# A ring of weight blocks, filled block by block instead of in four parts

## The reference

```python
h = silu(xn @ W1 * s1) * (xn @ W2 * s2)      # 256 -> 1024
h = gelu(h @ H1 * t1)                        # 1024 -> 1024
h = gelu(h @ H2 * t2)                        # 1024 -> 1024
ffn = h @ W3 * s3                            # 1024 -> 256
out = x + attention + ffn
```

## Time and profile before

| | |
|---|---|
| median of 3 runs | 1600.02 us |
| lowest, highest | 1595.21, 1600.1 us |
| profiled execution | 1599.94 us |
| its span | 1598.1 us |
| PE busy (matmuls) | 1520.8 us, 95% |
| DVE busy | 1169.4 us, 73% |
| ACT busy | 946.9 us, 59% |
| POOL busy | 481.8 us, 30% |
| DMA traffic | 298.16 MB, 84963 packets |
| of it GpSimd's queue | 238.04 MB, 37152 packets |

### The profile page before, as it was taken

The page is one execution under the profiler, slowest core; times in us unless marked ns, Lnnn a source line. Parts: engine busy times, 40 slices in busy tenths (PEclk is TensorE's granted clock), DMA queues, the critical chain, the costliest instruction groups (busy, mean ns, idle before and its releaser), DMA issues.

```text
span 1598.1 us, 33158 instructions
## 1 busy us (share of the span) xinstructions
PE 1520.8 (95%) x10956; PEld 1431.3 (90%) x10956; DVE 1169.4 (73%) x2087; ACT 946.9 (59%) x1745; POOL 481.8 (30%) x569
## 2 busy tenths in 40 slices
PE   7756999999999999999999999999999999999996
PEld 4756899998999999899999989999998999999896
DVE  4744686877868687786868778686877868686775
ACT  3523465665656566565656656565665656565563
POOL 1321051332405133240513324051332405133240
PEclk8977999999999999999999999999999999999999
DMA  8787356382745638274563827456382745737262
GB/s 298 257 302 265 120 174 236 101 274 75 256 153 170 235 103 272 77 256 153 169 234 104 268 81 256 153 165 236 106 267 82 257 152 163 239 105 249 88 228 86
DMA packets 84963, 298.16 MB, mean 187 GB/s; under 512 B 7232, under 2 KB 44224, under 8 KB 59584
## 3 DMA queue, kind: packets, MB, share of 16 engines
q0 software_dynamic: 37152, 238.04, 44.6%
q1 hardware_dynamic: 47344, 58.49, 11.3%
q10 hardware_dynamic: 432, 1.18, 0.2%
HBM read 280.91 MB, written 23.07 MB: 190 GB/s over the span
## 4 chain that ended last, share of the span: by engine, by line
PE 84%; DVE 6%; DMA 4%; issue 3%; ACT 2%; SPq 1%; POOL 1%; DVEq 0%; ACTq 0%; POOLq 0%
PE ps L833 48%; PE ps L808 13%; PE ps L862 8%; PE ps L713 4%; PE ps L714 4%; PE ps L715 4%; PE ps L753 2%; DMA weight_blocks<-in_w_ffn 2%; DVE values_a L1268 1%; DVE operands_a L1276 1%; DMA weight_set<-in_w_ffn 1%; PE ps L764 1%; PE ps L774 1%; PE ps L723 1%; DMA weight_blocks<-weight_set 1%
## 5 line engine op out<-in xcount | busy, mean ns | idle before, releaser
L833 PE MATMUL ps<-operands_a,hidden_weights 128*128 128x256 f32 x5376 | 697.8, 284 | 30.1 <-DVE operands_a L1276 13.4
L833 PEld LDWEIGHTS ps<-operands_a,hidden_weights 128*128 128x128 f32 x5376 | 665.4, 191 | 35.6 <-DVE operands_a L1276 17.0
L1299 DVE TENSOR_TENSOR partial_sums<-partial_sums,ps 128x512 f32<-128x512 f32 x320 | 218.1, 686 | 192.3 <-PE ps L833 128.8
L1276 DVE TENSOR_TENSOR operands_a<-values_a,operands_a 128x512 fp32r<-128x512 f32 x336 | 252.4, 770 | 57.6 <-POOL values_a L612 45.8
L618 POOL DMA_DIRECT2D hidden_weights<-weight_blocks x252 | 140.6, 558 | 495.9 <-PE ps L833 417.8
L833 PE MATMUL ps<-operands_b,hidden_weights 128*128 128x256 f32 x1792 | 256.8, 287 | 23.4 <-issue 11.2
L833 PEld LDWEIGHTS ps<-operands_b,hidden_weights 128*128 128x128 f32 x1792 | 233.4, 193 | 28.0 <-issue 18.0
L808 PE MATMUL ps<-xnT,w_ffn 128*128 128x512 f32 x1024 | 253.3, 399 | 0.0
L808 PEld LDWEIGHTS ps<-xnT,w_ffn 128*128 128x128 f32 x1024 | 189.3, 189 | 42.0
L1015 ACT ACTIVATE operands_a<-values_a 128x512 fp32r<-128x512 f32 x192 | 117.2, 628 | 70.3 <-POOL values_a L612 22.4
L1042 ACT ACTIVATE values_out<-partial_sums,vectors 128x256 f32<-128x256 f32 x192 | 87.0, 502 | 107.3 <-DVE partial_sums L1299 107.3
(11 more groups left out here) (108 smaller groups left out, 2076.7 us busy)
## 6 DMA issues: line engine op xcount, KB each, us to landing
hidden_weights<-weight_blocks POOLq DMA_DIRECT2D x192, 1024.0 KB, 5.3
hidden_weights<-weight_blocks POOLq DMA_DIRECT2D x64, 512.0 KB, 4.1
raw_weights<-weight_blocks SPq DMA_DIRECT2D x48, 272.0 KB, 2.7
x<-in_H SPq DMA_DIRECT2D x16, 512.0 KB, 5.5
weight_set<-in_w_ffn SPq DMA_DIRECT2D x16, 512.0 KB, 9.7
out_dram<-acc SPq DMA_DIRECT2D x32, 256.0 KB, 2.2
weight_blocks<-in_w_ffn SPq DMA_DIRECT2D x12, 512.0 KB, 14.7
weight_blocks<-weight_set SPq DMA_DIRECT2D x4, 1536.0 KB, 5.1
```

The costliest lines, as they stand in the source:

```text
L833: r = mm(bank[:, m * HT:(m + 1) * HT], ring_weights[:, place, 2 * g + j, m * P:(m + 1) * P], as_used(buf[:, j, slot[block_of_b], part, :]) ...
L1276: v.tensor_tensor(lo_part(group, block), value(group, block), hi_part(group, block).bitcast(F32), ALU.subtract).then_inc(lo_half.sem, 1)
L1299: v.tensor_tensor(scratch[:, dst, :], scratch[:, kept, :], product_bank(s, i), ALU.add).then_inc(add.sem, 1)
```

## The change

The ring gets seven parts of one block each, each with its own semaphore. Every refill waits for the one product whose block it replaces, and GpSimd's list has seven refills a step. They stand in groups where the four stood; in steps 1 and 3, where the products run in another order than the ring, the list follows the products' order, and in step 1 the refills of blocks 6 and 2 (R 1.2 and R 1.4) stand ahead of T4 of H0, the one of block 5 (R 1.1) behind it, with 7, 3 and 4.

```diff
 RING_ORDER = (1, 5, 6, 7, 2, 4, 3)
-RING_PARTS = ((0, 1), (1, 2), (3, 2), (5, 2))
-PART_OF = {1: 0, 5: 1, 6: 1, 7: 2, 2: 2, 4: 3, 3: 3}
+RING_PARTS = tuple((at, 1) for at in range(PRODUCTS))
+PART_OF = {i: at for at, i in enumerate(RING_ORDER)}
...
-PART_FREE = ((1, 6, 2, 3), (1, 5, 7, 4), (1, 6, 7, 3), (1, 5, 7, 4))
+PART_FREE = (RING_ORDER,) * SETS
...
                         refill(t, 0, 1)
                         refill(t, 0, 2)
+                        refill(t, 0, 3)
+                        refill(t, 0, 4)
                     t1(t, "H0")
                     t2(t, "H0")
                     if filling:
-                        refill(t, 0, 3)
+                        refill(t, 0, 5)
+                        refill(t, 0, 6)
...
                     if filling:
-                        refill(t, 1, 1)
+                        refill(t, 1, 2)
+                        refill(t, 1, 4)
                     if not staging:
                         t4(t, "H0")
                     if filling:
-                        refill(t, 1, 2)
+                        refill(t, 1, 1)
                         refill(t, 1, 3)
+                        refill(t, 1, 6)
+                        refill(t, 1, 5)
...
                         refill(t, 2, 1)
                         refill(t, 2, 2)
+                        refill(t, 2, 3)
+                        refill(t, 2, 4)
                     if staging:
                         ln1(t + 1)
                     if filling:
-                        refill(t, 2, 3)
+                        refill(t, 2, 5)
+                        refill(t, 2, 6)
                         if more:
                             refill(t, 3, 0)
+                            refill(t, 3, 2)
+                            refill(t, 3, 4)
                             refill(t, 3, 1)
-                            refill(t, 3, 2)
                             refill(t, 3, 3)
+                            refill(t, 3, 6)
+                            refill(t, 3, 5)
```

## The result

| | before | after |
|---|---|---|
| median | 1598.05 us (4 runs) | 1620.19 us (4 runs) |
| lowest, highest | 1595.21, 1600.1 us | 1619.14, 1620.59 us |
| profiled execution | 1599.94 us | 1620.59 us |
| its span | 1598.1 us | 1618.8 us |

The change costs 1.4%: the ratio is 1.0139, with a 95% interval of 1.0118 to 1.0159. The direction and the place were forecast, and 1620 lies in the range; the forecast's 11 us are half of the 22 measured.

What follows compares the result with a forecast made beforehand. TensorE's matmuls were taken to set the pace from tile 1 on. 1599.94 us plus 15 stalls of 0.7 us at block 5, plus 0 for tile 0, gave 1610.5, put at 1611; range 1604 to 1626 us.

Steps and rivals of the forecast that it cites:

- The range: Whole run: 1604 to 1626 us, holding the forecast's bounds, the GpSimd case and the lower part of the train.
- The forecast's own bounds: Whole run: 1607 to 1618 us, for block 5 landing 3.7 to 4.4 us after issue; chance 0.68.
- a late GpSimd: Rival, step 1's issues behind T4: the issue for product 4 slips, and H1's T4; 0.8 us more a tile, 1623; chance 0.05.
- a train that slows itself: Rival, step 1: blocks 7 and 3 following make block 5 land like a two-block load; 1.9 us a tile, 1629; chance 0.12.
- What bounds the kernel; nothing to gain: From tile 1 TensorE alone sets the pace; earlier weights can win at most 9.3 us, only in tile 0.
- The step 1 to 2: Block 5, issued behind H0's T4, goes out 3.54 us later, 3.29 us before product 5 of step 2 should start.
- The landing: Block 5's load in step 1: taken to land 3.9 us after issue, giving a stall of 0.7 us a tile.
- From the landing to the first matmul: Product 5 of step 2: TensorE starts 0.1 us after block 5's landing, a term of the stall.
- the sum of 1610.5: Whole run: 1599.94 us for the profiled execution + 15 × 0.7 + 0 for tile 0, put at 1611.
- GpSimd's list behind the four issues: Step 1 after T4: product 4's issue stays at 611.13 and H1's T4 at 615.05; margin about 0.3 us.
- Tile 0: Block 5 third in place of second, +1.4 us, taken up by the wait for H1's T4; sum 0, between −3 and +2.
- The skill's fit: One-block load: 2.0 us plus bytes over 436 GB/s, 3.2 us, stall about zero; supports the in-time rival, chance 0.13.

Runs made afterwards that it cites:

- e1: Kernel after the change, with block 5's refill in step 1 moved back ahead of H0's T4, seven one-block loads kept; 1600.83 us, ratio 1.0015 to before.
- e2: Kernel before, four loads a step kept, with the two-block load of 5 and 6 in step 1 issued behind H0's T4; 1632.24 us, ratio 1.0215.
- e5: Kernel after, with block 4's refill put between 5 and 7 in step 1, so nothing follows block 5 for 2.2 us; 1616.31 us, ratio 1.0123.
- e9: e1 with the same edit as e8, both T4 moved out from behind waits for copies; 1596.52 us, ratio 0.9994.
- e7: e1 with each load issued as two of 64 partitions, fourteen half loads a step, same bytes; 1700.81 us in one run.
- e8: Kernel before, with T4 of H0 and of H1 moved ahead of GpSimd's waits for weight copies in tile 0; 1591.67 us, ratio 0.9968.

## Why the prediction was right in its place and half its size

- **The range.** That 1620 lies in it is in part luck. The forecast's own bounds, to which it gave 0.68, end at 1618; the range reaches further because of two rivals, a late GpSimd and a train that slows itself, and neither of them happened.
- **What bounds the kernel; nothing to gain.** Right. The other six blocks have no wait in a steady tile, before or after, and e1 is not faster than before.
- **The step 1 to 2.** Right: T4 of H0 holds the issue, the waits all stand at product 5 of step 2, and issue to wanted start is 3.30 us where 3.29 was worked out. e1 and e2 show it from both sides.
- **The landing.** "I take 3.9, as the row for a block alone in the queue is the nearest case." That row was not the nearest: block 5 isn't alone. It landed after 4.1 us; 3.9 came back only in e5, where nothing follows. The median of 4.1 would have been the better choice. 0.2 us a tile.
- **From the landing to the first matmul.** 0.1 us was read off tile 0; in the steady tile it is 0.23. Tile 0 was the wrong place to read it: tile 0 and tile 15, which are written out, have 0.09 us, the tiles of the loop 0.23. No run shows what makes the difference. 0.1 us a tile.
- **A term left out.** The clock does hold at 1.00 after the stop in 14 of the 15 tiles (not in tile 8, below), as predicted, but the eight matmuls after it still take 0.1 us more. The same row was in the working (1.22 against 1.11 us) and was called "near".
- Together these three make the stall 1.1 us and not 0.7: 15 × 0.4 = 6 of the 10 us by which the profiled execution, 1620.59, exceeds the sum of 1610.5.
- **GpSimd's list behind the four issues.** Right: the issue for product 4 and T4 of H1 keep their distances to a hundredth of a microsecond. The rival had 0.05.
- **Tile 0.** Block 5's stop ends 1.7 us later (120.15 against 118.46; 1.4 were predicted), and the next, 4.48 us before, is 2.99, so most is taken up, as said. The refill ahead of T4 of H1 goes out 0.83 us later (128.63), and the tile ends 1.5 us later, inside the −3 to +2. One execution says little here: e2, whose tile 0 has the same list as before, took 150.3 us for it against 153.6. The medians speak against a sum of 0: of the 22.1 us between them, 15 stalls of 1.1 are 16.5 and GpSimd's stops 1.5, which leaves an estimated 4 us, by the interval of the ratio 1 to 7, for tile 0 and the end of the program; e1 and e9 give as much for the split. So the sum of 0 for tile 0 was probably some us too low, and that the wait for T4 of H1 covers the cost is not shown.
- **The skill's fit** (the Trainium skill, "DMA: Bandwidth & Descriptors", anatomy of a DMA) gave 3.2 us for one block and no stall. All 441 refills of the kernel after took 3.6 us or more, and block 5 took 4.1. The measurement decides against it. The same page's advice of 1 MiB or more per DMA for bandwidth (rules for kernel authors) is not what decided here either: e1 moves the same half-megabyte loads at no loss in a steady tile, and e2 loses more with the full ones.
- **Not foreseen:** the stop of GpSimd in tile 8, 3.4 us, while the 1.9 us of tile 14 went away. It explains 1.5 us of what the span grew by beyond 15 stalls, and it is told below. The rest in the profiled execution, 1.5 us of tile 0 and 1.0 of the last tile, is of the size by which single executions of this kernel differ; in the last tile a fall of the granted clock is part of it (below).

## What to carry over

Before a load is split or moved in a queue, find for each part the slack between its landing and its use, and look at what stands ahead of it in the issuing engine's list; a refill placed behind a compute instruction inherits that instruction's waits. Split and reorder in separate steps: here the order cost 1.1 us a tile, the split nothing in a steady tile, and together they looked like the price of smaller transfers. A stop that a price is said to hide behind should be taken away once: here that showed a faster kernel, and that most of the price had not been hidden.

## What the runs showed of the hardware that was not expected

**GpSimd stops for about 3.1 us every hundred-odd DMA issues.** In the sequencer's records of the traces it stands still for 3.1 to 3.3 us after 128 and 238 of its DMA issues in the kernel before, after 137, 243 and 348 in the kernel after, and in e7, which issues 896 and two more, after 174 and 288 and then after every 112 more, seven times in all. From one stop to the next are 105 to 114 issues in each of the three, but some 650, 365 and 200 us, and e7 moves the same bytes as the others; so what is counted goes with the issues, not with time or bytes. Two of e7's, two tiles apart:

```profile
387.07 4.11 POOL L617 DMA_DIRECT2D hidden_weights<-weight_blocks  x8 [3.63 <-issue]
...
587.39 4.11 POOL L617 DMA_DIRECT2D hidden_weights<-weight_blocks  x8 [3.58 <-issue]
```

What happens there isn't shown by any row. What it costs depends on where it falls. In the kernel before, one fell ahead of T4 of H1 in tile 14, and that tile is 1.9 us longer. In the kernel after, one fell in tile 8 right behind T4 of H0. GpSimd, then TensorE, then two windows of the stretch at the lower clock with two of tile 5 for comparison (PEclk is the third number from the end):

```profile
897.14 1.29 POOL L612 TENSOR_TENSOR values_b<-values_b 128x512 f32<-128x512 f32 x1 [2.99 <-DVE operands_b L1288]
900.27 2.33 POOL L618 DMA_DIRECT2D hidden_weights<-weight_blocks  x4 [1.84 <-PE ps L845]
```

```profile
904.58 2.07 PE L845 MATMUL ps<-operands_b,hidden_weights 128*128 128x256 f32 x8 [2.74 <-DMA hidden_weights<-weight_blocks]
906.45 1.80 PE L845 MATMUL ps<-operands_a,hidden_weights 128*128 128x256 f32 x8
```

```profile
904.58:906.45 1.87, 1.87 (x8) 1.87 (x9) 0.00 (x0) 0.74 (x2) 1.84 (x3) 0.50 1.12 405
906.45:908.09 1.64, 1.64 (x10) 1.64 (x9) 0.51 (x1) 1.40 (x3) 1.10 (x1) 0.53 1.11 367
619.55:620.60 1.05, 1.05 (x9) 1.05 (x9) 1.05 (x2) 0.91 (x2) 1.05 (x1) 1.00 1.15 425
620.60:621.55 0.95, 0.95 (x11) 0.95 (x10) 0.64 (x1) 0.83 (x2) 0.87 (x3) 1.00 1.12 414
```

Block 5 is issued 1.9 us late, and TensorE stops for 2.74 us in place of 0.83. After that longer stop the granted clock is 0.50, the lower of its two levels (1.2 GHz), for nearly all of two groups of eight matmuls, which take 1.87 and 1.64 us in place of 1.05 and 0.95: 1.5 us more. With the 1.9 us that makes tile 8 longer than the other tiles by its 3.4. After the stop of 0.83 us the clock stayed at 1.00.

The length of the stop alone doesn't decide it. In e2 TensorE stops for 1.8 to 2.2 us in each of tiles 1 to 14, and the clock stays at 1.00 after thirteen of these stops; after the one of tile 1 it falls, and the tile is 1.4 us longer than the others:

```profile
237.39 1.75 PE L832 MATMUL ps<-operands_b,hidden_weights 128*128 128x256 f32 x8 [1.84 <-DMA hidden_weights<-weight_blocks]
```

```profile
238.94:240.90 1.96, 1.96 (x11) 1.96 (x11) 0.69 (x1) 1.36 (x3) 0.46 (x1) 0.50 1.07 426
```

In the last tile the kernel before and the kernel after stop at the same place for the same time; the granted clock stays at 1.00 before and is 0.51 from 1539.4 to 1542.9 us after:

```profile
1519.59 2.64 PE L833 MATMUL ps<-operands_a,hidden_weights 128*128 128x256 f32 x20 [1.99 <-DVE operands_a L1276]
```

```profile
1538.16 3.61 PE L845 MATMUL ps<-operands_a,hidden_weights 128*128 128x256 f32 x20 [1.98 <-DVE operands_a L1288]
```

A stall of about 2 us thus cost its length in most cases and some 1.4 us more in a few. What separates them these runs don't show.

In e8 each of the tiles 1 to 14 is 93.3 us long, so no stop cost a tile anything there. The second one falls at the same place as in the kernel before, after 238 issues in tile 14, but T4 of H1 stands ahead of that refill now, and only the refills wait:

```profile
1447.31 1.30 POOL L612 TENSOR_TENSOR values_a<-values_a 128x512 f32<-128x512 f32 x1 [0.63 <-DVE operands_a L1276]
1450.56 1.15 POOL L618 DMA_DIRECT2D hidden_weights<-weight_blocks  x2 [1.96 <-PE ps L833]
```
